# Two heads' own-key products in one step, alternating between the heads' rows and banks, in layer 1's attention

## The chip, the cores and the metric

The kernel is one launch on one core of a Trainium2 chip. The time is the device time of one execution in microseconds; lower is better. The core's engines run side by side and meet only at semaphores: TensorE (PE; its weight loads are shown as PEld), VectorE (DVE), ScalarE (ACT), GpSimd (POOL) and SyncE (SP), which issues most of the DMAs.

## The reference, cut to what matters

Four layers, each a gated cross attention and a gated feed-forward network, on x of 8 batches x 256 tokens x 128 features with a context of 64 tokens a batch. The change touches the attention of layer 1 alone, in which the keys are those of the context and the tokens' own:

```python
def _L1_xattn_ref(x, x_text, Wq, Wk, Wv, gate, ln_g, ln_b, Wp, bp):
    q = x @ Wq.T
    k = jnp.concatenate([x_text @ Wk.T, x @ Wk.T], axis=1)   # 64 + 256 keys
    v = jnp.concatenate([x_text @ Wv.T, x @ Wv.T], axis=1)
    ...                                                      # 16 heads of 8
    scores = jnp.einsum('bhnd,bhkd->bhnk', q, k) / jnp.sqrt(jnp.float32(d))
    first = jnp.tanh(gate) * jnp.ones_like(scores[..., :1])
    rest = jax.nn.softmax(scores[..., 1:], axis=-1)
    attn = jnp.concatenate([first, rest], axis=-1)
    out = jnp.einsum('bhnk,bhkd->bhnd', attn, v)
    ...                                                      # layer norm
    return out @ Wp.T + bp
```

## The kernel before

The program is ten stages in a row (setup, then attention and feed-forward of layers 0 to 3, then the store), woven together at their seams. Each engine runs its own list of steps in order. A step waits for semaphores, issues its instructions, and its last one raises a semaphore. The list of an attention stage comes from a table by hand (`STEPS_1` for layer 1), which is run once a batch and holds pieces of neighbouring batches; further tables (`PLACES`) move single steps on one engine.

In layer 1 the 16 heads of a batch are worked on in four groups (g) of four heads. A head of a group has 32 of the 128 partitions, because its 8 features stand there in split form. For each group there are five score steps, `("scores", b, g, i)`:

- i = 0: the context's keys of all four heads. Two products over all 128 rows (line 709) fill one PSUM bank.
- i = 1 to 4: the own keys of head i. Two products, one for each half of the tokens, which use the 32 rows of that head alone (line 716), fill one bank of 512 columns.

VectorE then takes the maximum over each bank: line 1024 for i = 0 (into `mc`), line 1026 for i = 1 to 4 (into `ms`), and raises `sc_taken`. There are two banks for scores (`b_sc`, banks 2 and 3), used in turn. So a step waits until the one before the last has been taken, `sc_taken` of at + i - 1 with at = 5g: TensorE may fill one bank while VectorE reads the other.

When a group's five maxima are there, VectorE joins them (`mx`, line 1038). TensorE turns them (step `maxima`, line 731), ScalarE copies them (`hm`, line 887), and VectorE adds the queries (`hq`, 1049) and makes `mt` (1051). Then come five steps `("weights", b, g, i)`: the scores once more, with keys on the partitions, less the maximum: i = 0 for the context (756), i = 1 to 4 for one head each (767, heads in the order 2, 3, 4, 1). ScalarE takes the exponential of each bank (line 893, into `pt`) and raises `exp_done`. Here too are two banks in turn (`b_st`, banks 4 and 5), and step i waits for `exp_done` of at + i - 1. The step `pv` (798) multiplies with the values. The projection of the next batch's queries and keys (`proj`: 685 to 687 on TensorE, 880 on ScalarE, 1012 on VectorE), the turn of the outputs (815) and the layer norm run between these.

Of the kernel before, what the change touches and what calls it, by code (L numbers as in the profile page):

```python
# [17 lines left out]
P = 128  # L18
B, S, D, S2 = 8, 256, 128, 64
# [30 lines left out]
def need(eng, sem, value, past=0):  # L50

    if value > 0:
        eng.wait_ge(sem, past + value)
# [203 lines left out]
HEADS_1 = (0, 2, 3, 4, 1)  # L257
# [35 lines left out]
def attention(pr, layer, own_keys, masked, biased, scale, extra=None):  # L293
# [6 lines left out]
    U = NG * NS  # L300
# [22 lines left out]
    q = sb("q", [P, NG, S], F32R)  # L323
# [3 lines left out]
    mt = sb("mt", [P, 2, S], F32R)  # L327
# [6 lines left out]
    if own_keys:  # L334
        xt_raw = sb("xt_raw", [P, S])
        k = sb("k", [P, NG, S], F32R)
# [40 lines left out]
    sem, past = pr.sems(**raises)  # L377
# [3 lines left out]
    b_proj, b_turn, b_sc, b_st, b_mt, b_o = (pr.bank[0], pr.bank[1], pr.bank[2:4], pr.bank[4:6], pr.bank[6], pr.bank[7])  # L381
# [210 lines left out]
    def tensor(pe):  # L592
# [96 lines left out]

        def scores(b, g, i):  # L690
            at = g * NS
            need(pe, sem["sc_taken"], b * U + (at + i - 1), past["sc_taken"])
            o = b_sc[(at + i) % 2]
            if i == 0:
                pe.wait_ge(sem["qk_split"], past["qk_split"] + b * NG + g + 1)
                pe.wait_ge(sem["kc_ready"], past["kc_ready"] + b * NG + g + 1)
                if masked:
                    pe.wait_ge(sem["mk_split"], past["mk_split"] + b + 1)
                    if b == 0 and g == 0:
                        pe.wait_ge(sem["const_set"], past["const_set"] + 1)  # L700
                        pe.wait_ge(sem["xg_raw"], past["xg_raw"])
                    if b == 0 and g == 1:
                        pe.wait_ge(sem["vc_kept"], past["vc_kept"] + 2)
                if gated and b == 0 and g == 0:
                    pe.wait_ge(sem["h_done"], past["h_done"])
                    pe.wait_ge(sem["wf_ready"], past["wf_ready"] + 1)
                for t in range(2):
                    ts = slice(t * P, (t + 1) * P)
                    last = pe.matmul(o[:, t * S:(t + 1) * S], q[:, g, ts], kc[:, g], start=True, stop=not masked)  # L709
                    if masked:  # L710
                        last = pe.matmul(o[:, t * S:(t + 1) * S], msk[:, ts], i2[:, 0:S2].unsqueeze(1).to_broadcast([P, GH, S2]),
                                         start=False, stop=True)
            else:
                rows = slice(32 * (i - 1), 32 * i)
                for t in range(2):
                    last = pe.matmul(o[:, t * S:(t + 1) * S], q[rows, g, t * P:(t + 1) * P], k[rows, g], start=True, stop=True)  # L716
            last.then_inc(sem["sc_done"], 1)

        def maxima(b, g):
# [13 lines left out]

        def weights(b, g, i):
            at = g * NS
            need(pe, sem["exp_done"], b * U + (at + i - 1), past["exp_done"])
            o = b_st[(at + i) % 2]
            if i == 0:
                pe.wait_ge(sem["m_split"], past["m_split"] + b * NG + g + 1)
# [12 lines left out]
                for pair in range(2):  # L752
                    op = o[:, pair * S:(pair + 1) * S]
                    keys_of = kc[:, g, 2 * pair:2 * pair + 2].rearrange("p j s -> p (j s)")
                    if gated:
                        last = pe.matmul(op, keys_of, mt[:, g % 2], start=True, stop=True)
# [3 lines left out]
                        pe.matmul(op, i2[:], msk_all[:, bass.ds(b, 1)].rearrange("p a s -> p (a s)"), start=False, stop=False)  # L760
                    last = pe.matmul(op, selc[:, pair], mt[:, g % 2], start=False, stop=True)
            else:
                h = HEADS_1[i]
                rows = slice(32 * (h - 1), 32 * h)
                for kt in range(2):
                    op = o[:, kt * S:(kt + 1) * S]
                    last = pe.matmul(op, k[rows, g, kt * P:(kt + 1) * P], mt[rows, g % 2], start=True, stop=True)  # L767
            last.then_inc(sem["st_done"], 1)

        def values(b):  # L770
# [2453 lines left out]
```

## Time and profile before

| | us |
|---|---|
| median of 3 runs (lowest, highest) | 927.13 (927.07, 929.5) |
| profiled execution: time | 930.15 |
| profiled execution: span, first to last instruction | 928.4 |
| busy in the span: PE, DVE, ACT, POOL | 841.6, 763.0, 555.4, 309.8 |

The profiled execution lies 3.0 us above the median, and 1.8 us of it are outside the span. A group of instructions in a timeline is merged when nothing else of its engine comes between: its length goes from the first start to the last end. PE's busy time holds the pipeline's tail of each product, so that a busy PE isn't one at its peak. PEclk is the granted TensorE clock: 1.00 is 2.4 GHz and 0.50 is 1.2 GHz.

### The profile page before, as it was taken

To read this page: it belongs to the slowest core of one execution; us is meant where nothing else is said; L and a number is where in the kernel's file an instruction comes from. 1 tells how busy PE (TensorE), PEld (TensorE's weight loads), DVE (VectorE), ACT (ScalarE), POOL (GpSimd) and SP (SyncE) were. 2 spreads that over 40 slices of the span, in tenths; PEclk is the share of its full clock that TensorE was granted. 3 is DMA by queue.
4 is the path that set the end of the run, shared out by engine and by line. 5 is a ranking of instruction groups with operands and counts; after the bars stand their busy time and mean duration, and the time that the engine had idled before them with its cause. 6 is when DMAs were issued, how large, how long until landed. Compare 5 with 4: busy or idle time off the path is not lost.

```text
span 928.4 us, 16914 instructions
## 1 busy us (share of the span) xinstructions
PE 841.6 (91%) x5288; PEld 651.5 (70%) x5288; DVE 763.0 (82%) x1907; ACT 555.4 (60%) x1077; POOL 309.8 (33%) x507
## 2 busy tenths in 40 slices
PE   5998887899999999999999999999979989978796
PEld 3776756666666665688878788778767779867574
DVE  6899899869999998699889899788887755465886
ACT  3777565547777775675666565577755534423474
POOL 2644226313444433232222122433421253321143
PEclk9999999759999997999999999999998999997998
DMA  5000000000000000010000000020001000000001
GB/s 155 9 2 1 4 26 1 25 1 26 26 25 26 22 23 1 9 42 0 1 1 1 1 1 1 0 76 2 1 2 43 1 1 1 1 1 1 1 12 34
DMA packets 26005, 14.12 MB, mean 15 GB/s; under 512 B 11047, under 2 KB 25406, under 8 KB 25918
## 3 DMA queue, kind: packets, MB, share of 16 engines
q1 hardware_dynamic: 25758, 13.04, 5.1%
q8 instruction: 45, 0.74, 0.3%
q14 instruction: 42, 0.34, 0.1%
q10 hardware_dynamic: 160, 0.00, 0.0%
HBM read 11.99 MB, written 1.05 MB: 14 GB/s over the span
## 4 chain that ended last, share of the span: by engine, by line
PE 47%; DVE 8%; issue 3%; ACT 3%; POOL 0%; DVEq 0%; ACTq 0%; POOLq 0%
PE bank L1844 4%; PE bank L1846 3%; PE bank L1845 3%; PE bank L798 2%; PE bank L1319 2%; PE bank L1900 2%; PE bank L1901 2%; PE bank L1899 2%; PE bank L1274 2%; PE bank L1284 2%; PE bank L1297 1%; PE bank L1255 1%; PE bank L731 1%; PE bank L709 1%; PE bank L758 1%
## 5 line engine op out<-in xcount | busy, mean ns | idle before, releaser
L893 ACT ACTIVATE L_pt<-bank 128x512 f32<-128x512 f32 x224 | 127.2, 598 | 46.4 <-PE bank L767 32.5
L515 POOL TENSOR_TENSOR L_kc<-L_kc_all,const 128x256 fp32r<-128x256 f32 x96 | 59.7, 625 | 141.7 <-PE bank L767 81.9
L1026 DVE TENSOR_REDUCE L_ms<-bank 128x2 f32<-128x512 f32 x128 | 84.0, 685 | 11.8 <-PE bank L716 11.4
L1801 POOL TENSOR_TENSOR L1f_xg_lo<-L1f_xg_raw,L1f_xg_hi 128x512 fp32r<-128x512 f32 x32 | 42.0, 1313 | 145.3 <-ACT L1f_xg_hi L1949 141.3
L880 ACT ACTIVATE L_part<-bank,L_bias_ca,const 128x256 fp32r<-128x256 f32 x128 | 68.9, 563 | 33.8 <-PE bank L687 32.4
L2065 DVE TENSOR_TENSOR L1f_h_lo<-L1f_h,L1f_h_hi 128x512 fp32r<-128x512 f32 x88 | 75.2, 859 | 6.2 <-ACT L1f_h_hi L1954 5.9
L1943 ACT ACTIVATE L1f_a<-bank 128x512 f32<-128x512 f32 x88 | 52.4, 599 | 43.3 <-PE bank L1846 42.9
L1024 DVE TENSOR_REDUCE L_mc<-bank 128x8 f32<-128x512 f32 (+1 forms) x96 | 65.1, 678 | 8.7 <-PE bank L709 4.4
L1954 ACT CAST L1f_h_hi<-L1f_h 128x512 fp32r<-128x512 f32 x88 | 54.3, 618 | 18.8 <-DVE L1f_h L2060 18.8
L716 PE MATMUL bank<-L_k,L_q 32*128 32x256 f32 x256 | 55.9, 342 | 5.1 <-DVE L_ms L1026 4.9
L887 ACT ACTIVATE L_hm<-bank,const 128x256 fp32r<-128x256 f32 x96 | 45.6, 475 | 21.5 <-PE bank L731 20.6
L1012 DVE SCALAR_TENSOR_TENSOR L_q<-bank,L_bias_c,L_part 128x256 fp32r<-128x256 f32 x96 | 47.3, 493 | 11.9 <-ACT L_part L880 9.7
L709 PE MATMUL bank<-L_kc,L_q 128*128 128x256 f32 x192 | 48.9, 318 | 3.2 <-DVE L_ms L1026 2.1
L767 PE MATMUL bank<-L_mt,L_k 32*128 32x256 f32 x256 | 47.5, 351 | 4.6 <-ACT L_pt L893 3.8
L2060 DVE TENSOR_TENSOR L1f_h<-L1f_a,bank 128x512 f32<-128x512 f32 x64 | 43.6, 681 | 7.2 <-PE bank L1846 5.9
L685 PE MATMUL bank<-L_xt_hi,L_wx 128*128 128x256 f32 x128 | 43.8, 342 | 5.8 <-DVE L_q L1012 3.5
L767 PEld LDWEIGHTS bank<-L_mt,L_k 32*128 32x128 f32 x256 | 29.5, 203 | 26.8 <-ACT L_pt L893 15.1
L716 PEld LDWEIGHTS bank<-L_k,L_q 32*128 32x128 f32 x256 | 36.0, 202 | 16.7 <-DVE L_ms L1026 8.2
L731 PE MATMUL bank<-const,L_mx 128*128 128x128 f32 x192 | 40.9, 296 | 6.2 <-DVE L_mx L1040 2.1
L1844 PE MATMUL bank<-L1f_xt_hi,hi 128*128 128x512 f32 x112 | 45.3, 405 | 0.8 <-ACT L1f_a L1943 0.7
L1845 PE MATMUL bank<-L1f_xt_lo,hi 128*128 128x512 f32 x112 | 44.0, 393 | 0.0
L1846 PE MATMUL bank<-L1f_xt_hi,lo 128*128 128x512 f32 x112 | 44.0, 393 | 0.0
(427 smaller groups left out, 2601.1 us busy)
## 6 DMA issues: line engine op xcount, KB each, us to landing
L_raw<-in_L_ffn_w_dram SPq DMA_DIRECT2D x8, 176.0 KB, 2.3
L_raw<-in_L_ffn_v_dram SPq DMA_DIRECT2D x8, 176.0 KB, 2.5
L_raw<-in_L_ffn_w_dram SPq DMA_DIRECT2D x6, 192.0 KB, 2.9
x<-in_x_dram SPq DMA_DIRECT2D x4, 256.0 KB, 4.3
mask<-in_mask_Bx1xSxS_ff_dram SPq DMA_DIRECT2D x2, 512.0 KB, 5.6
out_dram<-x SPq DMA_DIRECT2D x4, 256.0 KB, 2.3
const<-in_const_dram SPq DMA_DIRECT2D x1, 964.0 KB, 6.0
ctx_rows<-in_ctx_dram SPq DMA_DIRECT2D x1, 256.0 KB, 3.1
```

What stands on the lines that cost most here:

```text
L515: pool.tensor_tensor(kc[:, g], kc_all[:, g, bass.ds(b, 1)].bitcast(F32).to_broadcast([P, GH, S2]), pr.c("head4").unsqueeze(2).to_broadcast ...
L709: last = pe.matmul(o[:, t * S:(t + 1) * S], q[:, g, ts], kc[:, g], start=True, stop=not masked)
L716: last = pe.matmul(o[:, t * S:(t + 1) * S], q[rows, g, t * P:(t + 1) * P], k[rows, g], start=True, stop=True)
L767: last = pe.matmul(op, k[rows, g, kt * P:(kt + 1) * P], mt[rows, g % 2], start=True, stop=True)
L880: last = act.activation(part[:, i].bitcast(F32R), b_proj[:, i * S:(i + 1) * S], ACT.Identity, bias=bias_ca[:, i, g:g + 1], scale=pr.c("ak" ...
L893: act.activation(pt[:, g // 2, (g % 2) * NS + (HEADS_1[i] if own_keys else i)], b_st[(g * NS + i) % 2][:], ACT.Exp, scale=scale).then_inc( ...
L1024: dve.tensor_reduce(mc[:].rearrange("p t j -> p (t j)"), by_head[:, :, start:], AX_X, ALU.max).then_inc(sem["sc_taken"], 1)
L1026: dve.tensor_reduce(ms[:, :, i - 1], bank.rearrange("p (t s) -> p t s", s=S), AX_X, ALU.max).then_inc(sem["sc_taken"], 1)
L1844: pe.matmul(bank[:], hi[:, at:at + P], xh, start=True, stop=False)
L1845: pe.matmul(bank[:], hi[:, at:at + P], xl, start=False, stop=False)
L1846: return pe.matmul(bank[:], lo[:, at:at + P], xh, start=False, stop=True)
L2065: dve.tensor_tensor(h_lo[:, r], h[:, r], h_hi[:, r].bitcast(F32), ALU.subtract).then_inc(sem["lo_done"], 1)
```

## The change

In both kinds of step, i = 1 now issues the products of i = 1 and i = 2, i = 3 those of 3 and 4, and i = 2 and 4 do nothing on TensorE. The four products go first half of the first head, first half of the second, second half of the first, second half of the second, so that neighbours differ in rows and in bank. The semaphores `sc_done` and `st_done` are still raised once a head. Since a step now fills both banks, it waits for `sc_taken` (`exp_done`) of at + i, where i = 1 and i = 3 waited for at + i - 1 before: until the bank of the step just before it has been read. VectorE's and ScalarE's own lists stay the same.

```diff
--- before.py
+++ after.py
@@ -689,7 +689,9 @@
 
         def scores(b, g, i):
             at = g * NS
-            need(pe, sem["sc_taken"], b * U + (at + i - 1), past["sc_taken"])
+            if i in (2, 4):
+                return
+            need(pe, sem["sc_taken"], b * U + (at + i - (0 if i else 1)), past["sc_taken"])
             o = b_sc[(at + i) % 2]
             if i == 0:
                 pe.wait_ge(sem["qk_split"], past["qk_split"] + b * NG + g + 1)
@@ -711,9 +713,12 @@
                         last = pe.matmul(o[:, t * S:(t + 1) * S], msk[:, ts], i2[:, 0:S2].unsqueeze(1).to_broadcast([P, GH, S2]),
                                          start=False, stop=True)
             else:
-                rows = slice(32 * (i - 1), 32 * i)
                 for t in range(2):
-                    last = pe.matmul(o[:, t * S:(t + 1) * S], q[rows, g, t * P:(t + 1) * P], k[rows, g], start=True, stop=True)
+                    for j in (i, i + 1):
+                        rows = slice(32 * (j - 1), 32 * j)
+                        last = pe.matmul(b_sc[(at + j) % 2][:, t * S:(t + 1) * S], q[rows, g, t * P:(t + 1) * P], k[rows, g], start=True, stop=True)
+                        if t == 1 and j == i:
+                            last.then_inc(sem["sc_done"], 1)
             last.then_inc(sem["sc_done"], 1)
 
         def maxima(b, g):
@@ -733,7 +738,9 @@
 
         def weights(b, g, i):
             at = g * NS
-            need(pe, sem["exp_done"], b * U + (at + i - 1), past["exp_done"])
+            if i in (2, 4):
+                return
+            need(pe, sem["exp_done"], b * U + (at + i - (0 if i else 1)), past["exp_done"])
             o = b_st[(at + i) % 2]
             if i == 0:
                 pe.wait_ge(sem["m_split"], past["m_split"] + b * NG + g + 1)
@@ -760,11 +767,12 @@
                         pe.matmul(op, i2[:], msk_all[:, bass.ds(b, 1)].rearrange("p a s -> p (a s)"), start=False, stop=False)
                     last = pe.matmul(op, selc[:, pair], mt[:, g % 2], start=False, stop=True)
             else:
-                h = HEADS_1[i]
-                rows = slice(32 * (h - 1), 32 * h)
                 for kt in range(2):
-                    op = o[:, kt * S:(kt + 1) * S]
-                    last = pe.matmul(op, k[rows, g, kt * P:(kt + 1) * P], mt[rows, g % 2], start=True, stop=True)
+                    for j in (i, i + 1):
+                        rows = slice(32 * (HEADS_1[j] - 1), 32 * HEADS_1[j])
+                        last = pe.matmul(b_st[(at + j) % 2][:, kt * S:(kt + 1) * S], k[rows, g, kt * P:(kt + 1) * P], mt[rows, g % 2], start=True, stop=True)
+                        if kt == 1 and j == i:
+                            last.then_inc(sem["st_done"], 1)
             last.then_inc(sem["st_done"], 1)
 
         def values(b):
```

On TensorE, in the middle of a batch, from the first product of a group's scores (L709 before, L711 in the changed kernel) through the own-key scores (L716, now L719), the turn of the last group's maxima (L731, now L736) and a projection. Before:

```order
L709 MATMUL bank3<-L1_kc,L1_q 128x256 x2
L716 MATMUL bank2<-L1_k,L1_q 128x256 x2
L731 MATMUL bank6<-const,L1_mx 128x128 x2
L685 MATMUL bank0<-L1_xt_hi,L1_wx 128x256
L686 MATMUL bank0<-L1_xt_lo,L1_wx 128x256
L687 MATMUL bank0<-L1_xt_hi,L1_wx 128x256
L685 MATMUL bank0<-L1_xt_hi,L1_wx 128x256
L686 MATMUL bank0<-L1_xt_lo,L1_wx 128x256
L687 MATMUL bank0<-L1_xt_hi,L1_wx 128x256
L716 MATMUL bank3<-L1_k,L1_q 128x256 x2
```

The same place in the changed kernel:

```order
L711 MATMUL bank3<-L1_kc,L1_q 128x256 x2
L719 MATMUL bank2<-L1_k,L1_q 128x256
L719 MATMUL bank3<-L1_k,L1_q 128x256
L719 MATMUL bank2<-L1_k,L1_q 128x256
L719 MATMUL bank3<-L1_k,L1_q 128x256
L736 MATMUL bank6<-const,L1_mx 128x128 x2
L685 MATMUL bank0<-L1_xt_hi,L1_wx 128x256
L686 MATMUL bank0<-L1_xt_lo,L1_wx 128x256
L687 MATMUL bank0<-L1_xt_hi,L1_wx 128x256
L685 MATMUL bank0<-L1_xt_hi,L1_wx 128x256
L686 MATMUL bank0<-L1_xt_lo,L1_wx 128x256
L687 MATMUL bank0<-L1_xt_hi,L1_wx 128x256
```

The second head's products have moved ahead of the turn of the maxima and the projection, into the step of head 1.

Right behind it, from `pv` (L798, now L806) through the last two score steps and the first two own-key weights (L767, now L773) to the turn of the outputs (L815, now L823). Before:

```order
L798 MATMUL bank7<-L1_pt,L1_vs 32x256 x8
L716 MATMUL bank2<-L1_k,L1_q 128x256 x2
L767 MATMUL bank4<-L1_mt,L1_k 128x256 x2
L767 MATMUL bank5<-L1_mt,L1_k 128x256 x2
L716 MATMUL bank3<-L1_k,L1_q 128x256 x2
L815 MATMUL bank1<-const,L1_ot 128x128 x4
```

The same place in the changed kernel:

```order
L806 MATMUL bank7<-L1_pt,L1_vs 32x256 x8
L719 MATMUL bank2<-L1_k,L1_q 128x256
L719 MATMUL bank3<-L1_k,L1_q 128x256
L719 MATMUL bank2<-L1_k,L1_q 128x256
L719 MATMUL bank3<-L1_k,L1_q 128x256
L773 MATMUL bank4<-L1_mt,L1_k 128x256
L773 MATMUL bank5<-L1_mt,L1_k 128x256
L773 MATMUL bank4<-L1_mt,L1_k 128x256
L773 MATMUL bank5<-L1_mt,L1_k 128x256
L823 MATMUL bank1<-const,L1_ot 128x128 x4
```

Heads 3 and 4 now stand together ahead of the weights, and head 4 no longer behind them.

## Rows read from the trace of the kernel before

**Rows 1.** The page: busy time by engine, and the chain by engine.
```profile
PE 841.6 (91%) x5288; PEld 651.5 (70%) x5288; DVE 763.0 (82%) x1907; ACT 555.4 (60%) x1077; POOL 309.8 (33%) x507
...
PE 47%; DVE 8%; issue 3%; ACT 3%; POOL 0%; DVEq 0%; ACTq 0%; POOLq 0%
```
**Rows 2.** Windows: length, busy (instructions) of each engine, PEclk, DMA share, GB/s.
```profile
162.50:172.50 10.00, 8.38 (x54) 6.48 (x52) 9.54 (x22) 5.06 (x11) 1.48 (x6) 1.00 0.01 2
172.50:206.60 34.10, 32.78 (x159) 22.61 (x158) 22.88 (x47) 17.86 (x37) 9.28 (x14) 0.50 0.06 17
253.60:278.30 24.70, 23.03 (x212) 15.69 (x210) 23.47 (x55) 18.48 (x38) 10.75 (x21) 1.00 0.09 25
```
**Rows 3.** Timeline of VectorE (start, us, line, out<-in): first reductions of head groups.
```profile
187.28 0.68 DVE L1024 TENSOR_REDUCE L_mc<-bank 128x8 f32<-128x504 f32 x1 [0.89 <-PE bank L709]
...
203.90 0.67 DVE L1024 TENSOR_REDUCE L_mc<-bank 128x8 f32<-128x504 f32 x1
...
243.92 0.65 DVE L1024 TENSOR_REDUCE L_mc<-bank 128x8 f32<-128x504 f32 x1
...
255.11 0.68 DVE L1024 TENSOR_REDUCE L_mc<-bank 128x8 f32<-128x504 f32 x1
...
279.75 0.68 DVE L1024 TENSOR_REDUCE L_mc<-bank 128x8 f32<-128x504 f32 x1
```
**Rows 4.** Timeline, all engines, 256.0 to 260.6.
```profile
256.01 0.50 PE L716 MATMUL bank<-L_k,L_q 32*128 32x256 f32 x4
...
257.99 2.56 DVE L1026 TENSOR_REDUCE L_ms<-bank 128x2 f32<-128x512 f32 x4
```
**Rows 5.** Timeline, 260.6 to 263.9.
```profile
260.61 0.50 PE L716 MATMUL bank<-L_k,L_q 32*128 32x256 f32 x2
...
261.04 0.44 PE L731 MATMUL bank<-const,L_mx 128*128 128x128 f32 x2
...
261.25 0.67 DVE L1024 TENSOR_REDUCE L_mc<-bank 128x8 f32<-128x504 f32 x1
261.39 0.39 PE L685 MATMUL bank<-L_xt_hi,L_wx 128*128 128x256 f32 x1
...
262.40 1.02 ACT L880 ACTIVATE L_part<-bank,L_bias_ca,const 128x256 fp32r<-128x256 f32 x2 [0.42 <-PE bank L687]
...
263.46 0.48 DVE L1012 SCALAR_TENSOR_TENSOR L_q<-bank,L_bias_c,L_part 128x256 fp32r<-128x256 f32 x1
```
**Rows 6.** Timeline, 263.7 to 266.5.
```profile
263.73 0.38 PE L716 MATMUL bank<-L_k,L_q 32*128 32x256 f32 x1
...
263.73 0.38 PE L767 MATMUL bank<-L_mt,L_k 32*128 32x256 f32 x1
...
264.25 1.96 DVE L1026 TENSOR_REDUCE L_ms<-bank 128x2 f32<-128x512 f32 x3
...
264.99 0.50 PE L716 MATMUL bank<-L_k,L_q 32*128 32x256 f32 x2 [0.53 <-DVE L_ms L1026]
...
266.00 0.51 PE L767 MATMUL bank<-L_mt,L_k 32*128 32x256 f32 x4
```
**Rows 7.** Timeline, 268.4 to 270.8.
```profile
268.38 0.50 PE L767 MATMUL bank<-L_mt,L_k 32*128 32x256 f32 x2
...
269.25 0.38 PE L767 MATMUL bank<-L_mt,L_k 32*128 32x256 f32 x1 [0.37 <-ACT L_pt L893]
...
270.28 0.47 ACT L887 ACTIVATE L_hm<-bank,const 128x256 fp32r<-128x256 f32 x1
```
**Rows 8.** Timeline, 276.1 to 278.4.
```profile
276.16 0.68 DVE L1026 TENSOR_REDUCE L_ms<-bank 128x2 f32<-128x512 f32 x1
...
277.07 1.29 DVE L1026 TENSOR_REDUCE L_ms<-bank 128x2 f32<-128x512 f32 x2 [0.22 <-PE bank L716]
```
**Rows 9.** Timeline, 167.4 to 171.6: the stage's first batch.
```profile
167.49 0.49 PE L716 MATMUL bank<-L_k,L_q 32*128 32x256 f32 x2 [0.35 <-DVE L_ms L1026]
...
171.06 0.50 PE L716 MATMUL bank<-L_k,L_q 32*128 32x256 f32 x2 [0.89 <-DVE L_ms L1026]
```

## The prediction

> **What bounds the kernel now.** I read the page's shares first and then left them. They point at TensorE: 91% busy against VectorE's 82%, and 47% of the chain that ended last [rows 1]. Both are averages over ten stages, and PE's share holds the tail of each product. The change lies in one stage, so the next view is the windows over it. In a batch in the middle of layer 1's attention VectorE is busy 23.47 of 24.70 us at a granted clock of 1.00 [rows 2]; it is idle 1.23 us. TensorE's 23.03 us there are tails and short waits too: its rows name VectorE's maxima as what they waited for, 0.53 us at 264.99 [rows 6]. A batch takes 279.75 - 255.11 = 24.64 us [rows 3]. So VectorE sets the pace of this stage while the clock is up, and what counts is whether its next bank is ready when it is free.
>
> The third thing to see is the clock. From 172.5 to 206.6 us it was 0.50, TensorE was busy 32.78 of 34.10 us and VectorE only 22.88 [rows 2]: there TensorE is the bound. The three first reductions from 187.28 to 203.90 span two head groups in 16.62 us; the same two groups take 243.92 to 255.11 = 11.19 us at full clock [rows 3], a factor of 1.49.
>
> **What alternating is worth.** Where both steps of a pair stood side by side and their banks were free, the hardware interleaved them already. Four own-key products took 0.50 us at 256.01 [rows 4], and four of the weights 0.51 us at 266.00; two alone took 0.50 us too [rows 6]. At 263.73 products of lines 716 and 767, of different heads, start together, though the second of line 716 stands between them in the program [rows 6]. So the new order within a pair is worth nothing where the steps were neighbours. By the list of TensorE, 5 of 8 score pairs and 1 of 8 weight pairs of a batch were apart; since four take as long as two, joining a pair saves at most the 0.50 us of two products: 6 x 0.50 = 3.0 us a batch of TensorE's time, and nothing of the end while VectorE is the bound.
>
> The Trainium skill ("TensorE: Matmul & The Clock Gate", Part 3) says that weight loads overlap with products in flight only where the row group differs, but that products start in program order. By the first half alternating would pay in every pair; the trace shows the overlap but not the strict order, and so leaves only the six pairs that stood apart.
>
> **What the wait costs.** The new step needs both banks, so its first product waits until VectorE has read the step just before. The reaction time: of the three reductions in 1.96 us from 264.25, one lasting 0.68 [rows 6, 8], the first ends at 264.93; the products that waited for it start at 264.99 and last 0.50, and the third reduction, which needs them, starts at 264.25 + 1.96 - 0.68 = 265.53, that is 0.60 us after the first's end. Reductions that find their bank full overlap: two take 1.29 us where each lasts 0.68 [rows 8], so 0.07. Each place where VectorE goes straight from step 0 to 1, or from 2 to 3, loses 0.60 + 0.07 = 0.67 us. VectorE's list has four such places in a batch. I go through one batch; the head groups are named by their first reduction.
>
> - Group at 255.11. Steps 1 and 2 are issued at 256.01, long before VectorE asks: nothing. Steps 1 to 4 are reduced without a break from 257.99 [rows 4], so a break of 0.67 comes in before step 3; of the batch's 1.23 us of idle time I let 0.14 take it up: 0.53.
> - Group at 261.25, steps 1 and 2. Step 1's products went at 260.61 [rows 5]; now they wait for the reduction that ends at 261.92, and with them the turn of the maxima (261.04) and the projection (261.39), which stand behind in TensorE's list. With the spacings of those rows: pair at 261.98, turn 0.43 later at 262.41, projection 0.35 later at 262.76 against 261.39. From the projection to VectorE's work on q it is 263.46 - 261.39 = 2.07 us by way of ScalarE's part [rows 5]; q moves from 263.46 to 264.83: 1.37 in all, 0.67 of it the break itself.
> - Same group, steps 3 and 4. Three reductions stand in one row of 1.96 us at 264.25 [rows 6], a break before the second: 0.67. TensorE stands meanwhile, and the weights, moved behind the pair, come late for ScalarE.
> - The next group. The weights of heads 1 and 2 of the list went at 268.38 and 269.25, the second behind ScalarE's exponential [rows 7]; now both wait for it, 0.87 later. The exponentials and `hm` (270.28) follow in ScalarE's list, and VectorE's hq behind `hm`. About 0.5 of the 0.87 reaches VectorE after its own lateness is taken off.
> - The last group of the four. Steps 1 and 2 are hidden by hq and mt; before step 3 another break of 0.67; VectorE already waited 0.22 in that group at 277.07 for its bank [rows 8], which falls away: 0.45.
>
> Sum: 0.53 + 1.37 + 0.67 + 0.5 + 0.45 = 3.5 us a batch, 24.64 to 28.2. Lower bound: the four breaks alone less all idle time of VectorE, 4 x 0.67 - 1.23 = 1.5 us. Upper bound: every one of the eight score pairs pays 0.67, 5.4 us. I take 3.5, since it follows the rows one by one.
>
> At full clock run some 6.4 of the 8 batches (206.6 to about 365): 6.4 x 3.5 = 22 us. The other 1.6, at half clock, are bounded by TensorE: the joined pairs give it up to 3.0 us a batch and the waits take up to 3.5; I take +2 us in all, between -5 and +6. So 24 us by waits; the bounds are 6.4 x 1.5 - 5 = 5 and 6.4 x 5.4 + 6 = 41.
>
> **The clock.** In the first batch the pattern of the new waits stands already in the trace: products waiting 0.35 us at 167.49 and 0.89 us at 171.06 for a maximum [rows 9], TensorE busy 8.38 of 10.00 us, and then the clock fell at 172.5 [rows 2]. The change makes such waits in every batch (261.98 - 260.61 = 1.4 us, and 264.99 - 263.73 = 1.3 us for the next pair, even without its own lateness). So I expect another stretch at 0.50 about as long as the one that is there: 34.1 x (1 - 1/1.49) = 11 us. Bounds: -11 if the present stretch goes, and 6.4 x 24.64 x 0.49 = +77 if the clock stays down.
>
> Sum: 24 + 11 = 35 us on the profiled execution's own time, 930.15 + 35 = 965. That execution lies 3.0 us above the median, 927.13, so the forecast is 962 us. Nothing else issues or moves: no DMA, and the lists of DVE, ACT, POOL and SP keep their order.
>
> The Trainium skill ("TensorEngine Tiling (Array Packing)", PSUM Bottleneck) warns that tiling speeds up TensorE but not the emptying of PSUM. The trace agrees: VectorE, which empties these banks, is the one at 95% in a batch. By that rule alone the change would give 0.
>
> **The rivals.**
> - The clock stays at 0.50 for half of the stage or more. For it: it took from 172.5 to 206.6 us to come back, with TensorE always busy. Against: nothing in the 6.4 batches after that made it fall, waits of 0.53 included. Price: 24 + 39 to 77 us, so 990 to 1028, 1000 for half of it and a little more.
> - Slack hides the waits. The breaks fall into VectorE's 1.23 us of idle time and TensorE catches up 3.0 us a batch through the joined pairs. Then 0 to 1.5 us a batch, at most 12: 927 to 938. Against: VectorE can't catch up at 95%.
> - TensorE is the bound after all, as the page has it, and the joined pairs are the price: faster. 8 x 3.0 = 24 us at most, 903; where TensorE gains at half clock alone, or the clock comes back earlier, 915 to 924, and I put this rival at 918. It decides if VectorE's next bank is what TensorE delivers late at nearly every reduction. Against: three and four reductions without a break [rows 4, 6].
> - The pairing does nothing (the hardware interleaves anyway, and waits fall where TensorE waited before): 927.
>
> **How the numbers follow.** My forecast, 940 to 985 us, has 0.47. The clock staying down has 0.25, the slack 0.11 (over 930 us for two thirds), the faster rival 0.11, no effect 0.06. Two runs of this kernel differ by about 0.3% (3 us), so within that is "the same". Faster: 0.11. The same: 0.06 and the rest of the slack case, 0.09. Slower: 0.80. The range of 8 in 10 takes the forecast's, most of the slack case and half of the clock's: 932 to 1008.
>
> **What would show it.** Right: VectorE's time on line 1026 the same, but idle time before it that names PE bank, about 4 places a batch at 0.6 us; batches of 28 us between first reductions; products of line 716 and 767 (719 and 773 now) always in fours of 0.50 us. The clock: a second stretch at 0.50 within the stage. Wrong: batches still of 24.7 us (slack), shorter ones (TensorE), or a loss at full clock above 5.4 us a batch, which would mean that PE and ACT, not VectorE's breaks, took over.

## The result, and the profile after

The changed kernel took 981.47 us (median of 4 runs, 975.39 to 996.16), the kernel before 927.37 (4 runs on the same chip, 927.07 to 929.5). The ratio is 1.0556, with a 95% interval of 1.0498 to 1.0614. That is slower by 54 us; 962 had been forecast, so the direction was right and the loss was 1.5 times as large. Ratios here leave out a run that is over 1.5% above the fastest of its kernel, while medians keep it, so the two differ a little in e7 and e11. The profiled execution is the longest of the four, 996.16 us with a span of 994.4 us, at a granted clock of 0.888 where the other three had 0.910 to 0.916; stage times below are from it, and they are some 15 us too long for the median.

The page of the changed kernel, against [rows 1]: busy time by engine, then the chain by engine, then two of the costliest groups (busy us, mean ns of one, idle time before them and who ended it).

```profile
PE 878.2 (88%) x5288; PEld 673.9 (68%) x5288; DVE 768.9 (77%) x1907; ACT 555.5 (56%) x1077; POOL 309.5 (31%) x507
...
PE 67%; DVE 16%; ACT 8%; issue 6%; POOL 1%; ACTq 1%; DVEq 0%; POOLq 0%
...
L1034 DVE TENSOR_REDUCE L_ms<-bank 128x2 f32<-128x512 f32 x128 | 83.9, 685 | 47.4 <-PE bank L719 47.2
...
L719 PE MATMUL bank<-L_k,L_q 32*128 32x256 f32 x256 | 49.7, 398 | 28.2 <-DVE L_mc L1032 21.0
```

The same two groups on the page of the kernel before:

```profile
L1026 DVE TENSOR_REDUCE L_ms<-bank 128x2 f32<-128x512 f32 x128 | 84.0, 685 | 11.8 <-PE bank L716 11.4
...
L716 PE MATMUL bank<-L_k,L_q 32*128 32x256 f32 x256 | 55.9, 342 | 5.1 <-DVE L_ms L1026 4.9
```

The counts are the same, 5288 products and 1907 instructions of VectorE, and so is the work of a maximum, 685 ns. New is the idle time: VectorE stands 35.6 us more ahead of the maxima, waiting for the own-key scores, and TensorE stands 23.1 us more ahead of those scores, waiting for VectorE. Each waits for the other; that is a handshake that has lost its lookahead.

Windows over the stage, from the first to the last of the 32 first reductions of layer 1's attention (length, busy and instructions of each engine, granted clock, DMA share, GB/s), and under it four that follow one another in its middle:

```profile
163.80:424.20 260.40, 219.82 (x1500) 147.13 (x1500) 182.07 (x396) 137.46 (x281) 69.52 (x136) 0.68 0.05 16
...
303.30:310.10 6.80, 5.22 (x54) 3.42 (x55) 6.18 (x15) 4.51 (x9) 0.61 (x1) 1.00 0.16 52
310.20:320.40 10.20, 10.20 (x62) 7.40 (x58) 6.69 (x19) 5.46 (x11) 1.34 (x2) 0.50 0.01 3
320.50:327.20 6.70, 4.68 (x48) 2.89 (x41) 4.04 (x8) 3.48 (x8) 0.61 (x1) 1.00 0.00 0
327.30:337.40 10.10, 9.19 (x58) 5.74 (x58) 7.69 (x18) 5.17 (x11) 7.04 (x15) 0.50 0.09 25
```

The same stage of the kernel before:

```profile
163.10:359.40 196.30, 183.07 (x1504) 124.95 (x1502) 176.02 (x396) 136.69 (x281) 69.46 (x136) 0.91 0.07 21
```

Nearly the whole difference lies here: 260.4 - 196.3 = 64.1 us, against 994.4 - 928.4 = 66.0 us of the spans. There are two parts to it. The clock is the first: before it is 0.50 for 34 us, once [rows 2]; now it falls again and again. From about 276 to 378 us it goes up for 6.8 us and down for 10.2 in turn. At full clock TensorE is busy 5.22 of 6.80 us and 4.68 of 6.70, at half clock 10.20 of 10.20 and 9.19 of 10.10.

The second part shows only where the clock is up. Late in the stage it is, and the timeline has two of the breaks that were forecast (start, us, engine, line; in brackets the idle time before and who ended it):

```profile
412.15 0.67 DVE L1032 TENSOR_REDUCE L_mc<-bank 128x8 f32<-128x504 f32 x1
...
412.88 0.51 PE L719 MATMUL bank<-L_k,L_q 32*128 32x256 f32 x4 [1.63 <-DVE L_mc L1032]
...
415.47 0.69 DVE L1034 TENSOR_REDUCE L_ms<-bank 128x2 f32<-128x512 f32 x1 [0.66 <-PE bank L719]
...
417.75 0.68 DVE L1032 TENSOR_REDUCE L_mc<-bank 128x8 f32<-128x504 f32 x1
...
422.62 1.29 DVE L1034 TENSOR_REDUCE L_ms<-bank 128x2 f32<-128x512 f32 x2 [0.64 <-PE bank L719]
...
424.22 0.68 DVE L1032 TENSOR_REDUCE L_mc<-bank 128x8 f32<-128x504 f32 x1
```

The four products start 0.06 us after the reduction that frees their bank (412.15 + 0.67 = 412.82) and last 0.51, for all four. Where before three or four maxima ran in one row [rows 4, 6], or stopped for 0.22 us [rows 8], VectorE now stands 0.64 to 0.66 us between them. The two intervals between first reductions are 5.60 and 6.47 us; before, the same two took 4.99 and 6.14 (250.12 and then 255.11 and 261.25 of [rows 3, 5]).

**Two parts from the clocks alone.** Each run has a mean granted clock, so its time at half clock can be had without a trace: 2 x (1 - clock) x time. Before: 2 x 0.047 x 928 = 87 us. After, at the median clock of 0.911: 2 x 0.089 x 981 = 175 us. At half clock this stage's work takes 1.49 times as long [rows 3], so of 88 us more, 88 x (1 - 1/1.49) = 29 us are the clock's doing. The other 54 - 29 = 25 us are waits at a given clock. It is an estimate: 1.49 comes from two head groups of the kernel before. The spread of the runs gives the same price: from 975.39 to 996.16 us the changed kernel's clock goes from 0.916 to 0.888, which is 164 to 223 us at half clock, so 0.35 us of time for each of them, where 1 - 1/1.49 is 0.33. In the profiled execution the same sum gives 133 x 0.33 = 44 of the stage's 64 us to the clock and leaves 20. In the experiments below "the clock's part" is worked out in this way.

### The profile page after: what moved, and what is told of

Same layout as the page of the kernel before. It is cut to its first block, busy times and chain, and to the rows that moved or that the text cites. A ratio compares the mean times of both kernels' runs of the same rounds, so it can differ in the third digit from the quotient of the medians.

```text
span 994.4 us, 16914 instructions
## 1 busy us (share of the span) xinstructions
PE 878.2 (88%) x5288; PEld 673.9 (68%) x5288; DVE 768.9 (77%) x1907; ACT 555.5 (56%) x1077; POOL 309.5 (31%) x507
## 4 chain that ended last, share of the span: by engine, by line
PE 67%; DVE 16%; ACT 8%; issue 6%; POOL 1%; ACTq 1%; DVEq 0%; POOLq 0%
PE bank L806 5%; PE bank L1852 4%; PE bank L773 4%; PE bank L1853 3%; PE bank L1854 3%; PE bank L719 3%; ACT L_pt L901 3%; PE bank L711 3%; PE bank L736 2%; PE bank L685 2%; DVE L_mc L1032 2%; ACT L_part L888 2%; PE bank L1908 2%; PE bank L1907 2%; PE bank L687 2%
## 5 line engine op out<-in xcount | busy, mean ns | idle before, releaser
L1034 DVE TENSOR_REDUCE L_ms<-bank 128x2 f32<-128x512 f32 x128 | 83.9, 685 | 47.4 <-PE bank L719 47.2
L719 PE MATMUL bank<-L_k,L_q 32*128 32x256 f32 x256 | 49.7, 398 | 28.2 <-DVE L_mc L1032 21.0
L1020 DVE SCALAR_TENSOR_TENSOR L_q<-bank,L_bias_c,L_part 128x256 fp32r<-128x256 f32 x96 | 47.4, 494 | 25.1 <-ACT L_part L888 24.3
L719 PEld LDWEIGHTS bank<-L_k,L_q 32*128 32x128 f32 x256 | 33.9, 249 | 41.0 <-DVE L_mc L1032 25.8
L773 PE MATMUL bank<-L_mt,L_k 32*128 32x256 f32 x256 | 44.9, 418 | 11.5 <-ACT L_pt L901 11.5
L711 PE MATMUL bank<-L_kc,L_q 128*128 128x256 f32 x192 | 51.6, 334 | 2.4 <-DVE L_ms L1034 1.4
L773 PEld LDWEIGHTS bank<-L_mt,L_k 32*128 32x128 f32 x256 | 28.7, 256 | 36.3 <-ACT L_pt L901 27.3
L685 PE MATMUL bank<-L_xt_hi,L_wx 128*128 128x256 f32 x128 | 48.5, 379 | 5.4 <-DVE L_q L1020 3.5
L806 PE MATMUL bank<-L_pt,L_vs 128*32 128x256 f32 x512 | 49.7, 509 | 0.0
L736 PE MATMUL bank<-const,L_mx 128*128 128x128 f32 x192 | 42.7, 307 | 5.7 <-DVE L_mx L1048 2.1
## 6 DMA issues: line engine op xcount, KB each, us to landing
x<-in_x_dram SPq DMA_DIRECT2D x4, 256.0 KB, 4.0
out_dram<-x SPq DMA_DIRECT2D x4, 256.0 KB, 2.3
ctx_rows<-in_ctx_dram SPq DMA_DIRECT2D x1, 256.0 KB, 3.1
```

What stands on the lines that cost most here:

```text
L685: pe.matmul(o, wx[:, 2 * i, cols], xt_hi[:], start=True, stop=False)
L719: last = pe.matmul(b_sc[(at + j) % 2][:, t * S:(t + 1) * S], q[rows, g, t * P:(t + 1) * P], k[rows, g], start=True, stop=True)
L773: last = pe.matmul(b_st[(at + j) % 2][:, kt * S:(kt + 1) * S], k[rows, g, kt * P:(kt + 1) * P], mt[rows, g % 2], start=True, stop=True)
L806: last = pe.matmul(out, lhs, rhs, start=(i == 0), stop=(i == NS - 1))
L1034: dve.tensor_reduce(ms[:, :, i - 1], bank.rearrange("p (t s) -> p t s", s=S), AX_X, ALU.max).then_inc(sem["sc_taken"], 1)
```

## The experiments

Twelve kernels ran. Each was timed beside the kernel before on its own chip, so ratios are the thing to compare. "Stage" is the same stretch as above in the profiled execution.

### What of the change costs: e1 to e5

**e1, the pairs joined but not alternating.** The joined step of the changed kernel, with the first head's two products and then the second's:

```diff
-                for t in range(2):
-                    for j in (i, i + 1):
+                for j in (i, i + 1):
+                    for t in range(2):
```

> Both steps of a pair in one place and behind the joint wait, but the two heads' products one head after the other instead of alternating. Theory W (the cost is the joint wait and what it does to the clock; alternating is worth nothing, since neighbouring steps were interleaved by the hardware before): within 1% of the changed kernel, 972 to 990. Rival A (alternating rows and banks itself costs or gains, for instance by weight loads that no longer hide): away from the changed kernel by more than 1.5%, below 966 or above 996.

Measured: 983.13 us, ratio 1.0601 (1.0523 to 1.0678), within the error of the full change, which is about 1%. Alternation is worth nothing that these runs can see, in either direction. This run also has the clock up for most of a batch, so it shows all four breaks. Its timeline of VectorE, and the products behind the third first reduction:

```profile
305.06 0.69 DVE L1034 TENSOR_REDUCE L_ms<-bank 128x2 f32<-128x512 f32 x1 [0.64 <-PE bank L719]
...
307.36 0.68 DVE L1032 TENSOR_REDUCE L_mc<-bank 128x8 f32<-128x504 f32 x1
...
312.20 1.29 DVE L1034 TENSOR_REDUCE L_ms<-bank 128x2 f32<-128x512 f32 x2 [0.61 <-PE bank L719]
...
314.11 0.67 DVE L1032 TENSOR_REDUCE L_mc<-bank 128x8 f32<-128x504 f32 x1
...
314.84 0.51 PE L719 MATMUL bank<-L_k,L_q 32*128 32x256 f32 x4 [1.33 <-DVE L_mc L1032]
315.27 0.44 PE L736 MATMUL bank<-const,L_mx 128*128 128x128 f32 x2
315.37 0.69 DVE L1034 TENSOR_REDUCE L_ms<-bank 128x2 f32<-128x512 f32 x1 [0.59 <-PE bank L719]
...
317.95 0.48 DVE L1020 SCALAR_TENSOR_TENSOR L_q<-bank,L_bias_c,L_part 128x256 fp32r<-128x256 f32 x1 [0.81 <-ACT L_part L888]
...
320.01 1.29 DVE L1034 TENSOR_REDUCE L_ms<-bank 128x2 f32<-128x512 f32 x2 [0.59 <-PE bank L719]
...
323.51 0.65 DVE L1032 TENSOR_REDUCE L_mc<-bank 128x8 f32<-128x504 f32 x1
```

Four breaks of 0.64, 0.61, 0.59 and 0.59 us, in the four places named. The fifth wait, 0.81 us before q, is the list of TensorE standing: turn of the maxima and projection stood behind the four products (and the clock fell at about 316 us, in the projection). The four groups of a batch take, with group 1's 5.60 and the 6.69 of group 0 elsewhere in the trace, the following:

| group to the next | before | forecast | e1 |
|---|---|---|---|
| 0 to 1 | 6.19 | 6.7 | 6.69 |
| 1 to 2 | 4.97 | 5.4 | 5.60 |
| 2 to 3 | 6.17 | 6.7 | 6.75 |
| 3 to the next 0 | 7.34 | 9.38 | 9.40 |
| batch | 24.7 | 28.2 | 28.4 |

(The last interval of e1 lies partly at half clock: 0.82 on average. At full clock e2 has 9.02 us for it, and e7, with one pair joined, 9.04.)

**e2, the old waits.** In the joined step each head waits for its own bank only, as before the change; the places in TensorE's list stay the new ones, and nothing alternates:

```diff
-            need(pe, sem["sc_taken"], b * U + (at + i - (0 if i else 1)), past["sc_taken"])
+            need(pe, sem["sc_taken"], b * U + (at + i - 1), past["sc_taken"])
...
+                    if j > i:
+                        need(pe, sem["sc_taken"], b * U + (at + i), past["sc_taken"])
```

(and the same for the weights, with exp_done).

> Pairs in their new place, not alternating, but each head waits for its own bank alone, as before (at + i - 1 for each). So VectorE and ScalarE have their next bank ahead again; what stays is that the second head's wait now stands ahead of steps that it stood behind before. Theory W: most of the loss goes; the four breaks of 0.67 us a batch vanish and with them part of the low clock: 930 to 950. Rival P (the place: it is what stands behind the pair in TensorE's list that is late, not the break): 960 to 985, as the changed kernel.

Measured: 983.68 us, ratio 1.0555 (1.0489 to 1.0621). The breaks of VectorE that I had priced one by one are gone, and nothing comes back. Group 3 in its timeline:

```profile
348.92 0.67 DVE L1036 TENSOR_REDUCE L_mc<-bank 128x8 f32<-128x504 f32 x1
...
349.51 0.68 DVE L1038 TENSOR_REDUCE L_ms<-bank 128x2 f32<-128x512 f32 x1
...
349.65 0.50 PE L721 MATMUL bank<-L_k,L_q 32*128 32x256 f32 x2 [0.63 <-DVE L_mc L1036]
350.08 0.44 PE L738 MATMUL bank<-const,L_mx 128*128 128x128 f32 x2
...
351.06 0.42 DVE L1061 TENSOR_TENSOR L_hq<-L_hm,L_q 128x256 f32<-128x256 f32 x1 [0.87 <-ACT L_hm L899]
...
352.31 0.48 DVE L1024 SCALAR_TENSOR_TENSOR L_q<-bank,L_bias_c,L_part 128x256 fp32r<-128x256 f32 x1 [0.37 <-ACT L_part L892]
...
353.11 1.96 DVE L1038 TENSOR_REDUCE L_ms<-bank 128x2 f32<-128x512 f32 x3
...
357.94 0.65 DVE L1036 TENSOR_REDUCE L_mc<-bank 128x8 f32<-128x504 f32 x1
```

The break of VectorE is gone: 349.51 follows the first reduction at once, and three maxima run in one row again. But the second head's products still stand ahead of the turn of the maxima, waiting 0.63 us, so VectorE stands 0.87 us ahead of hq and 0.37 ahead of q, and the group takes 9.02 us (9.40 in e1, 7.34 before). The batch is 27.5 us long. So, as far as group 3 shows, the wait and the place are two ways to the same delay, not two terms: whichever holds TensorE until VectorE's reduction is over delays all that stands behind in the list.

**e3, the scores alone, and e4, the weights alone.** Each takes one half of the change and leaves the other function as it was:

```diff
         def weights(b, g, i):
-            if i in (2, 4):
-                return
-            need(pe, sem["exp_done"], b * U + (at + i - (0 if i else 1)), past["exp_done"])
+            need(pe, sem["exp_done"], b * U + (at + i - 1), past["exp_done"])
```

> The change for the scores alone; the weights' steps as before. Theory W with VectorE as the bound: nearly the whole loss, 965 to 985. Rival S (ScalarE's exponentials behind the weights' pairs carry it): 930 to 945.

> The change for the weights alone; the scores' steps as before. Theory W: ScalarE has slack (busy 18.5 of 24.7 us a batch) and hides it nearly: 927 to 938. Rival S: 955 or more.

Measured: scores alone 978.21 us, ratio 1.051 (1.0455 to 1.0565), stage 246.1 us; weights alone 941.73 us, ratio 1.0138 (1.0092 to 1.0183), stage 204.8 us. The scores are nearly the whole loss. The weights' part at full clock is a batch of 25.3 us, 0.6 more than before, where the forecast had 0.5; in whole runs it is 11 us, 4 of them the clock's part, above the 927 to 938 that I had put on it.

**e5, the new wait alone.** Each head's scores stay a step of their own, at the old place in the list; the first of a pair waits for both banks, as if it were joined:

```diff
-            need(pe, sem["sc_taken"], b * U + (at + i - 1), past["sc_taken"])
+            need(pe, sem["sc_taken"], b * U + (at + i - (0 if own_keys and i in (1, 3) else 1)), past["sc_taken"])
```

(own_keys is set where the step is of layer 1.)

> The kernel before with one thing changed: score steps 1 and 3 wait for sc_taken of at + i, as the changed kernel's do, but every product stays in its old place, one head a step, and the weights stay as they were. Breaks and whatever stands behind steps 1 and 3 in TensorE's list are hit; what stands between the two steps of a pair isn't moved behind the second head. Theory V (VectorE's four breaks are a real part of the cost): 4 x 0.67 less some idle time, 1.5 to 3.4 us a batch at full clock, 950 to 975. Rival P (the place of the second head's products is the cost; the run with the old waits in the new place already took the whole loss): under 1 us a batch, 927 to 940.

Measured: 991.76 us against 932.09, ratio 1.0664 (1.0597 to 1.073), stage 254.2 us. Its page, the group of the maxima:

```profile
PE 47%; DVE 9%; issue 3%; ACT 3%; POOL 0%; DVEq 0%; ACTq 0%; POOLq 0%
...
L1026 DVE TENSOR_REDUCE L_ms<-bank 128x2 f32<-128x512 f32 x128 | 85.0, 687 | 51.7 <-PE bank L716 51.6
```

The wait by itself costs all of it and a little more. Idle time before the maxima is 51.7 us, against 11.8 before and 47.4 after. The first line is a warning about a view: the chain's shares by engine are, to a point, those of the fast kernel [rows 1], though this one is 60 us slower; PE's 67% in the changed kernel told nothing either. Together with e2: the wait at the old place costs the whole loss, and so does the new place with the old wait. e5 is above the full change, by 1% in ratio, and the traces have a place where that arises. The head groups 0 and 1 of the second batch lie wholly at a clock of 0.50 in each kernel: together they take 16.62 us before [rows 3], 17.56 in the changed kernel (194.91 to 212.47) and 18.84 in e5 (196.56 to 215.40). So the wait costs time at half clock too, and the joined pairs give part of it back there. That this makes up the whole 1% is not shown.

### Which pairs: e6, e7, e10

**e6, only pairs that stood together.** Three score pairs of a batch were neighbours in TensorE's list and had both banks free early. These alone are joined and alternate:

```diff
+            near = (g, i) in ((0, 1), (0, 3), (2, 1))
+            if (g, i - 1) in ((0, 1), (0, 3), (2, 1)):
+                return
+            need(pe, sem["sc_taken"], b * U + (at + i - (0 if near else 1)), past["sc_taken"])
...
+                    for j in ((i, i + 1) if near else (i,)):
```

> The change for the three score pairs a batch whose steps stood side by side in TensorE's list already (group 0, heads 1 and 2, heads 3 and 4; group 2, heads 1 and 2), with the joint wait and alternating; all else as before. In none of these goes VectorE straight from the first step to the pair. Alternating worth nothing and no break: 924 to 931, same as before. Rival A (alternating helps, or hurts, by itself): out of 918 to 936.

Measured: 931.57 us against 932.09, ratio 0.9999 (0.9978 to 1.0021), 10 runs. The intervals at full clock are 6.20, 4.97, 6.17 and 7.34 us, those of the kernel before to 0.01. Alternation is worth nothing where the pairs were neighbours already, and joining costs nothing where the banks are free.

**e7, one far pair.** Of all pairs only that of group 3, heads 1 and 2, is joined (the edit of e6 with the set `((3, 1),)`).

> The change for one score pair a batch alone: group 3, heads 1 and 2, the pair that the prediction priced highest (1.37 us a batch, from group 3's first reduction on). By my walk the interval from group 3's first reduction to the next batch's grows from 7.3 to 8.7 us at full clock, 8 batches make 11 us, and the waits at two places may cost a clock stretch more: 936 to 950. Rival (the loss needs all pairs, TensorE catches one up): 927 to 932.

Measured: 946.63 us, ratio 1.0128 (1.0067 to 1.0189). Group 3 in its timeline, with the first reduction that ends it:

```profile
323.50 0.67 DVE L1030 TENSOR_REDUCE L_mc<-bank 128x8 f32<-128x504 f32 x1
...
324.23 0.50 PE L720 MATMUL bank<-L_k,L_q 32*128 32x256 f32 x4 [1.31 <-DVE L_mc L1030]
...
324.77 0.69 DVE L1032 TENSOR_REDUCE L_ms<-bank 128x2 f32<-128x512 f32 x1 [0.59 <-PE bank L720]
...
326.91 0.48 DVE L1018 SCALAR_TENSOR_TENSOR L_q<-bank,L_bias_c,L_part 128x256 fp32r<-128x256 f32 x1 [0.38 <-ACT L_part L886]
...
329.70 0.84 DVE L1044 TENSOR_TENSOR L_mx<-L_mc,L_ms 128x16 f32<-128x16 f32 x1
...
332.54 0.65 DVE L1030 TENSOR_REDUCE L_mc<-bank 128x8 f32<-128x504 f32 x1
```

332.54 - 323.50 = 9.04 us, 1.70 more than before, where the forecast had 1.37. q comes 326.91 - 323.50 = 3.41 us behind the first reduction, 1.20 later than before (263.46 - 261.25 = 2.21 [rows 5]). The rest arises behind it: `mx` lasts 0.84 us, where it lasted 0.24 before; why is not shown. The other three groups of this batch are unchanged. In four other batches the clock falls for 3.4 us at the end of group 3 (as from 301.9 to 305.3 us), and the next group 0, at full clock again, takes 7.1 us instead of 6.2.

**e10, the same pair, issued later.** The joined pair goes out at the second head's old place, behind the turn of the maxima and the projection:

```diff
+            near = (g, i) == (3, 2)
+            if (g, i) == (3, 1):
+                return
...
+                    for j in ((i - 1, i) if near else (i,)):
```

> One score pair a batch, group 3, heads 1 and 2, as in the run with one far pair, but issued at the place of its second step, behind the turn of the maxima and the projection; the joint wait costs TensorE nothing there, since the second head waited for the same. What is left is that the first head's scores come late for VectorE. In the trace before, the pair's place is 262.30 and step 1 was reduced at 261.84: it would start at about 262.83, 1.0 us later, and q isn't held up further. Theory L (what stands behind the wait in TensorE's list is the larger part of the cost): the interval of group 3 grows by 1.0 at most against 1.7 with the early place, 932 to 940, faster than the run with one far pair (946.6). Rival D (VectorE's break is the cost, wherever the pair stands): as that run, 943 to 950.

Measured: 944.09 us against 931.27, ratio 1.0171 (1.0097 to 1.0244).

```profile
353.16 0.67 DVE L1030 TENSOR_REDUCE L_mc<-bank 128x8 f32<-128x504 f32 x1
...
354.21 0.50 PE L720 MATMUL bank<-L_k,L_q 32*128 32x256 f32 x4
354.74 0.69 DVE L1032 TENSOR_REDUCE L_ms<-bank 128x2 f32<-128x512 f32 x1 [0.91 <-PE bank L720]
...
361.30 0.65 DVE L1030 TENSOR_REDUCE L_mc<-bank 128x8 f32<-128x504 f32 x1
```

The group takes 8.14 us here (8.24 in most batches), 0.9 more than before, and q no longer waits. VectorE's stop ahead of step 1 is longer than e7's, 0.91 against 0.59 us, since the pair stands behind the projection, and it is the whole cost. So of the 1.7 us of e7, 0.8 go when nothing stands behind the pair. The interval was as expected; the total was not. With 0.8 us less in each batch the run should be 5 us shorter than e7, and no gain shows: in both, the clock spends more time down (2 x (1 - 0.9395) x 944 = 114 us against 91 before, so 8 us of e10's 13 are the clock's part). The runs of each spread over 14 to 16 us with the clock (937.4 to 953.8 in e7, 938.6 to 952.5 in e10), and four of each can't tell 5 us. The windows over the stage, of e7 and of e10:

```profile
164.30:376.10 211.80, 188.77 (x1502) 130.17 (x1501) 181.28 (x397) 136.94 (x281) 69.88 (x136) 0.87 0.07 19
```

```profile
163.90:382.10 218.20, 202.30 (x1502) 137.44 (x1501) 177.79 (x397) 136.28 (x281) 69.71 (x136) 0.80 0.06 19
```

Before, the clock of the stage was 0.91, and it never fell after the first batches. One long wait in a batch is enough to bring new falls: e7's TensorE waits 1.31 us, e10's 1.29, where the kernel before has no wait above 0.6 us in those batches.

### The clock: e8, e9, e11, e12

**e8 and e9, products at the waits.** The changed kernel, and at the five places of a batch where the pair waits, 8 (e9: 4) extra products with 128 rows into the pair's free bank. They leave TensorE less idle; what they write is overwritten by the pair:

```diff
+                for n in range(8 if (g, i) in ((1, 1), (1, 3), (2, 3), (3, 1), (3, 3)) else 0):
+                    pe.matmul(b_sc[(at + i) % 2][:, (n % 2) * S:(n % 2 + 1) * S], q[:, g, (n % 2) * P:(n % 2 + 1) * P], kc[:, g], start=True, stop=True)
+                need(pe, sem["sc_taken"], b * U + (at + i), past["sc_taken"])
```

> The changed kernel with eight more products over all 128 rows (query times context keys, 256 columns) in front of the five score pairs a batch that wait longest; they write the bank that is free already and that the own keys' products overwrite, and stand ahead of the wait for the second bank. They take 0.9 us of TensorE where it stood still. Theory C (about half of the loss, some 25 to 30 us, is the granted clock, which falls because of the waits): the clock stays at 1.00 in the stage more, 950 to 965, faster than the changed kernel though 320 products are added. Rival (the clock is not moved by it, or the products cost what they take): 980 to 1000.

> The changed kernel with four additional products, not eight, in front of the same five score pairs a batch. With eight the clock stayed up (0.954) but a batch took 30.3 us at full clock in its trace, 2.1 us more than the pairs alone. Theory C (the waits cost 3.5 us a batch, the clock about as much again): if four still hold the clock, 28.2 to 29 us a batch and 958 to 970. Rival (four are too few): clock 0.91 to 0.93 and 972 to 985.

Windows over the stage, of e8:

```profile
163.00:404.20 241.20, 215.06 (x1808) 155.33 (x1808) 177.14 (x396) 136.81 (x281) 69.58 (x136) 0.92 0.06 17
```

and of e9:

```profile
163.10:411.20 248.10, 214.86 (x1657) 149.27 (x1657) 178.81 (x397) 137.47 (x281) 69.45 (x136) 0.84 0.06 16
```

Measured: e8 976.93 us, ratio 1.0487 (1.0456 to 1.0517); e9 982.33, ratio 1.0562 (1.0505 to 1.062). The clock did what the idea said: 0.92 in the stage with eight products and 0.84 with four, against 0.68 after and 0.91 before. The time did not: I had expected 950 to 965 for e8. Its batch at full clock is 30.3 us long where e1's is 28.4. The rows say where the fillers (line 697) hurt:

```profile
300.85 1.21 PE L697 MATMUL bank<-L_kc,L_q 128*128 128x256 f32 x8
...
302.52 0.69 DVE L1038 TENSOR_REDUCE L_ms<-bank 128x2 f32<-128x512 f32 x1 [1.98 <-PE bank L723]
...
312.09 1.22 PE L697 MATMUL bank<-L_kc,L_q 128*128 128x256 f32 x8
...
313.24 0.50 PE L723 MATMUL bank<-L_k,L_q 32*128 32x256 f32 x4
```

The fillers at 312.09 cost nothing: the first reduction ends at 313.17, and the pair starts 0.07 us later. Those at 300.85, ahead of heads 3 and 4 of group 1, start when both banks are free already (the maxima before them ended at 300.54), and VectorE stands 1.98 us instead of 0.64. The same holds in group 2 (1.95 us). These two groups are 1.1 and 1.2 us longer than e1's, more than the whole excess; fillers at the other three places alone were not tried. With the clock of the kernel before, e8 is 45 us slower than it: none of that is the clock's, so in e8 all is waits and fillers. It shows that the clock depends on what TensorE does at these waits, and that fillers at these five places don't buy the clock's part back.

**e11 and e12, products in the first batch of the kernel before.** The 34 us at half clock in the kernel before follow the waits of its first batch [rows 9]. Here 2 (e12: 4) extra products stand ahead of score steps 1 and 2 of groups 1 to 3 and of every own-key weight step of that batch, nothing of the change being in:

```diff
+                for n in range(4 if b == 0 and g and i < 3 else 0):
+                    pe.matmul(o[:, (n % 2) * S:(n % 2 + 1) * S], q[:, g, (n % 2) * P:(n % 2 + 1) * P], kc[:, g], start=True, stop=True)
```

(e12's, for the scores; the weights have the like.)

> The kernel before, with two additional products over 128 rows ahead of each own-key weights step of the first batch and ahead of the score steps 1 and 2 of its groups 1 to 3, into the bank that the step overwrites. The clock was at 0.50 from 172.5 to 206.6 us, in the first batch, where TensorE has less to do. If it stays up there, up to 11 us come back less what the products cost: 918 to 930. Rival (it falls all the same, or a little later): 930 to 937.

> The same with four additional products a step: 916 to 928 if they hold the clock, 932 to 945 if they only make TensorE's first batch longer.

Measured: e11 938.81 us, ratio 1.0028 (0.999 to 1.0066); e12 931.50, ratio 1.0024 (0.9989 to 1.0059), 10 runs each. With two products the clock still fell for 48 us in the stage of e11's profiled execution (943.15 us), which had 0.88 on average. The stage of e12:

```profile
163.10:360.30 197.20, 185.17 (x1592) 128.57 (x1590) 175.65 (x397) 137.06 (x281) 69.32 (x136) 1.00 0.07 21
```

The clock never falls in it, and the stage is as long as before: 197.2 against 196.3 us. The extra products cost what the clock gives back. So neither beats the kernel before, and nor does any other version here.

## Why the forecast was right in direction and short in size

**VectorE sets the pace: right.** Had TensorE been the bound, as its share of 91% [rows 1] suggests, joined pairs would have made the kernel faster. e1's batch of 28.4 us against 24.7 excludes that rival. That VectorE is the one that sets the pace rests on its 23.47 busy us of 24.70 [rows 2] and on e7 and e10, where stops of VectorE of 0.59 and 0.91 us go with a group longer by 1.70 and 0.90; no run made either engine's work shorter.

**Alternation is worth nothing: right,** shown by e1 and e6. Rows 4 and 6 had said so: four products in the time of two, without help of the program.

**A break of 0.67 us in four places: right in place,** 0.59 to 0.66 us in each. The whole batch came out at 28.4 us against 28.2 (e1), and the waits' part of the loss at 25 us against 24. In part that is luck: e1's last group lies partly at half clock, the 25 is what an estimate leaves over, and the sum had a wrong form, as follows. For the batches at half clock the sum had +2 us; the two groups measured there, 17.56 against 16.62 us, agree in sign.

**The terms as a sum: wrong in form.** I had added breaks of VectorE and delays of TensorE's list as if each could be taken away alone. e2 takes the breaks away and has 27.5 us; e5 keeps the old places and is no faster. For group 3's first pair by itself (e7) the break is 0.59 us where I had 0.67, q is 1.20 late where I had 1.37, and the group is 1.70 longer, so that some 0.5 us arise behind q, where the sum has no term; issued late (e10) the pair costs 0.9. In e2 the break goes and the group still takes 9.02 us, as in e7.

**The clock: right in direction, the term that was too small.** The term was "another stretch at 0.50 about as long as the one that is there", 11 us. Measured by the clocks of the runs it is about 29, and in the profiled execution about 44. The rival had the other end, half of the stage or more at 0.50; the trace has 167 us of 260 at 0.50, so its picture was nearer than mine; its price, 990 to 1028, was reached by the profiled execution (996) and not by the median, which has 25 + 29 us. I had argued "one more stretch" from one event at 172.5 us, and against more with "nothing in the 6.4 batches after that made it fall, waits of 0.53 included". Those batches did not have waits of 1.3 us in them, as e7's have. The row that was closest stood in my own list: 0.89 us of idle time at 171.06, and then the fall at 172.5 [rows 2, 9]. The change was to put waits of that kind into every batch, so falls in every batch were the reading at hand, not one in the stage.

**What stays open.** What exactly makes the clock fall is not shown: the runs say that waits of TensorE bring it (e5, e7) and products at the waits hold it (e8, e12), not how long or how often. Runs of one kernel also differ by up to 2% with it, as 975 to 996 us after. And how much of e5's extra over the full change arises at half clock is not measured.

## What to carry to other kernels

Before you join two steps that write two buffers in turn, look whether the reader of those buffers is the bound: with two banks, a joint step can't start before the reader has let go of both, and each place where the reader goes from one bank straight to the next then costs it the producer's whole reaction time (0.6 us here). Count as well what stands behind the joint step in its engine's list, and don't add the two: removing one may leave the other in full. And where the producer is TensorE, price the idle time twice, once as a wait and once in granted clock: here, by the estimate above, the second was as dear as the first.

## What was not expected of the hardware

- Small products of different row groups start out of their order in the program, or together: 716 and 767 at 263.73 [rows 6], though the second product of 716, which stands ahead of 767 in the list, starts only at 263.95; and four of the joined pair last 0.51 us whether they alternate or not (412.88 after, 314.84 in e1).
- The clock can swing with a steady beat: 6.8 us up and 10.2 us down for about 100 us, while every batch does the same work. TensorE is busy 91 to 100% of the low stretches shown and 70 to 77% of the high ones.
- What a fall of the clock costs can show behind it: in e7 the falls of 3.4 us lie in group 3, which takes 9.02 us with and 9.04 without one, and it is the group after them, at 1.00 again, that takes 7.1 us instead of 6.2.
- A longer group of 1.7 us (e7), 11 us in the stage (6.4 x 1.7), made the kernel some 12 us slower (ratio 1.0128), and one of 0.9 us (e10) made it 13 slower by the medians. The runs differ too much among themselves to rank the two.
